# Memory attention on one core: scores and values issued by octets of heads instead of quads, exponentials a quad further ahead, and the projection chunks dealt anew

## The reference

```python
xn = layernorm(x) * ln_g + ln_b
q = heads(xn @ Wq); k, v = heads(xn @ Wkv)     # 16 heads of 64
mem = heads(ctx @ Wm)                          # 77 context rows
k = concatenate([k, mem]); v = concatenate([v, mem])   # 128 + 77 = 205 keys
attn = softmax(q @ k.T * 64 ** -0.5)
x = x + heads_joined(attn @ v) @ Wo + bo
```

## Time and profile before

| | |
|---|---|
| median of 3 runs | 3393.23 us (3392.61 to 3394.02) |
| the profiled execution, its span | 3395.16 us, 3393.4 us |
| memory attention | about 586 to 2014 us of the span |
| busy over the span: PE, DVE, ACT, POOL | 91%, 72%, 68%, 43% |
| busy in 640 to 1960 us: PE, DVE, ACT | 1299, 1017, 872 of 1320 us |

### The profile page before, as it was taken

How to read it: one execution, slowest core, us unless ns; L and a number is a source line. 1 busy time by engine, 2 the same in 40 slices (tenths; PEclk the granted TensorE clock), 3 DMA queues, 4 the chain that set the end, 5 groups by cost and what they waited for, 6 DMA issues and landing times. The chain is left out here.

```text
span 3393.4 us, 98827 instructions
## 1 busy us (share of the span) xinstructions
PE 3088.2 (91%) x27585; PEld 2273.9 (67%) x27741; DVE 2434.0 (72%) x8135; ACT 2315.4 (68%) x8950; POOL 1453.9 (43%) x2636
## 2 busy tenths in 40 slices
PE   7999997999999999999999968879979999968776
PEld 4555555788888888888888855657746666644444
DVE  6888886677777777777777751136657888868886
ACT  6888886666666666666666643337759999965554
POOL 5777775112222212222222210026647777746775
PEclk9999998999999999999999989989989999989999
DMA  4000001000000000000000002310000000000000
GB/s 147 0 0 0 0 0 58 23 4 5 5 5 5 5 5 5 5 3 5 5 5 4 4 5 81 83 49 18 17 9 7 5 6 5 5 3 7 12 17 14
DMA packets 80369, 54.43 MB, mean 16 GB/s; under 512 B 24801, under 2 KB 74413, under 8 KB 80160
## 3 DMA queue, kind: packets, MB, share of 16 engines
q1 hardware_dynamic: 76192, 45.27, 4.7%
q0 software_dynamic: 4096, 8.16, 0.8%
HBM read 32.67 MB, written 20.97 MB: 16 GB/s over the span
## 5 line engine op out<-in xcount | busy, mean ns | idle before, releaser
L873 DVE COPY b_prT<-b_tr 128x512 f32<-128x512 f32 x512 | 352.1, 688 | 237.8 <-PE b_tr L765 233.6
L1131 ACT ACTIVATE b_pr<-b_sc,b_low 128x205 f32<-128x205 f32 x1024 | 431.0, 431 | 33.9 <-DVE b_low L849 33.9
L461 ACT ACTIVATE a_pr<-a_sc,a_low 128x128 f32<-128x128 f32 x1024 | 360.8, 386 | 12.0 <-DVE a_low L364 7.2
L864 DVE TENSOR_SCALAR b_pn<-b_pr,b_rec 128x205 f32<-128x205 f32 x1024 | 298.8, 334 | 54.8
L1188 POOL TENSOR_TENSOR b_ln_var<-b_ln_mean_var,all_eps 128x1 f32<-128x1 f32 x64 | 12.1, 190 | 757.9 <-DVE b_ln_mean_var L140 757.9
L765 PE MATMUL b_tr<-all_ident,b_pn 128*128 128x128 f32 x2048 | 323.3, 281 | 5.3 <-DVE b_prT L873 3.1
L2108 ACT ACTIVATE f_pr<-f_sc,f_low 128x77 f32<-128x77 f32 x1024 | 320.2, 338 | 10.0 <-DVE f_low L1999 2.8
L500 POOL TENSOR_TENSOR a_pn<-a_pr,a_rec 128x512 f32<-128x512 f32 x256 | 261.2, 1042 | 123.4 <-DVE a_rec L372 106.7
L765 PEld LDWEIGHTS b_tr<-all_ident,b_pn 128*128 128x128 f32 x2048 | 227.5, 141 | 86.9 <-issue 78.8
L849 DVE TENSOR_REDUCE b_low<-b_sc 128x4 f32<-128x820 f32 x256 | 256.3, 1002 | 9.5 <-PE b_sc L753 9.5
L753 PE MATMUL b_sc<-b_kT,b_q 64*128 64x205 f32 x2048 | 247.1, 359 | 0.0
(11 more groups left out here) (302 smaller groups left out, 8494.7 us busy)
## 6 DMA issues: line engine op xcount, KB each, us to landing
scratch_x<-b_zeros SPq DMA_DIRECT2D x12, 512.0 KB, 5.0
e_xr<-scratch_x SPq DMA_DIRECT2D x24, 256.0 KB, 3.0
scratch_y<-e_yr SPq DMA_DIRECT2D x24, 256.0 KB, 2.4
all_X<-in_x SPq DMA_DIRECT2D x8, 512.0 KB, 6.9
e_w<-in_e_w SPq DMA_DIRECT2D x16, 256.0 KB, 3.1
out_x<-all_X SPq DMA_DIRECT2D x8, 512.0 KB, 3.2
w_mask<-in_mask SPq DMA_DIRECT2D x1, 2464.0 KB, 11.1
b_cT<-in_ctxT SPq DMA_DIRECT2D x32, 77.0 KB, 2.0
```

The lines of the kernel that those rows point to most:

```text
L461: op = act.activation(pr[:, g, u], sc[:, g, 128 * u:128 * u + 128], ACT.Exp, bias=low[:, g, u:u + 1], scale=-1.0, accum_out=sums[:, g, u:u ...
L864: op = dve.tensor_scalar(pn[:, j % 2, g, 0:KN], pr[:, j % 2, g, 0:KN], rec[:, j % 2, g:g + 1], None, ALU.mult)
L873: dve.tensor_copy(prT[:, j % 2, i].rearrange("p h t q -> p (h t q)"), tr[:]).then_inc(prT_made, 1)
L1131: op = act.activation(pr[:, j % 2, g, 0:KN], sc[:, j % 2, h, KN * i:KN * i + KN], ACT.Exp, bias=low[:, j % 2, g:g + 1], scale=-1.0, accum_ ...
```

## The change

Within the same stage, and with the same arithmetic:

- `score` takes an octet (two quads) at once and is issued twice a step instead of four times, in turns 0 and 2; it now waits until both quads in sc are exponentiated. `values` takes an octet too, also in turns 0 and 2.
- `exponentials` works two quads ahead instead of one, so b_low, b_sums, b_rec and b_pr have four buffers, as has b_prT.
- The values of an octet fill the whole bank b_pm (512 columns), and the projected output p_y is written into the first 128 columns of that bank, where it had columns of its own. `project_out` stands in turn 1 instead of turn 0, `residual` in turn 1 of VectorE, and the values of the next octet wait for it.
- `lowest` of both quads of an octet stands in turns 0 and 2, on either side of the second `divide`.
- The chunks are dealt anew, `place` moves ahead of the second k, and the router's `choose` moves from turn 2 to turn 1.

```diff
-        po, p_y = pm[:, 0:256], pm[:, 256:384]
+        po, p_y = pm, pm[:, 0:128]
...
-                  [("xT", 0), ("q", 0), ("k", 0), ("q", 1), ("k", 1), ("mv", 0), ("v", 0), ("v", 1), ("mv", 1),
-                   ("place", 0), ("rT", 0), ("rT", 1)]]
-
-        EARLY = [[[0, 1], [4, 5], [8], [11]], [[0], [], [4], []]]
-        LATE = [[[2, 3], [6, 7], [9, 10], [12, 13]], [[1], [2, 3], [5, 6], [7, 8, 9, 10, 11]]]
+                  [("xT", 0), ("q", 0), ("k", 0), ("q", 1), ("place", 0), ("k", 1), ("mv", 0), ("v", 0), ("v", 1),
+                   ("mv", 1), ("rT", 0), ("rT", 1)]]
+
+        EARLY = [[[], [2, 3, 4, 5], [], [9, 10, 11]], [[0], [2], [4], [6, 7]]]
+        LATE = [[[0, 1], [6, 7], [8], [12, 13]], [[1], [3], [5], [8, 9, 10, 11]]]
...
-                def score(b, p, j):
-                    n = NJ * b + j
-                    if due(2 * n - 2):
-                        pe.wait_ge(exped, 2 * n - 2)
...
+                def score(b, p, o):
+                    n = NJ * b + 2 * o
+                    if due(2 * n):
+                        pe.wait_ge(exped, 2 * n)
...
+                    for j in (2 * o, 2 * o + 1):
+                        for i in range(2):
+                            for h in range(2):
...
+                        last.then_inc(scored, 1)
...
                     for j in range(NJ):
                         transposes(b, j, 0)
+                        if j == 1 and not first:
+                            project_out(b - 1, 1 - p)
...
-                        if j > 0:
-                            values(b, p, j - 1)
-                        elif not first:
-                            values(b - 1, 1 - p, NJ - 1)
-                        if j < 2:
-                            score(b, p, j + 2)
-                        elif not last:
-                            score(b + 1, 1 - p, j - 2)
+                        if j == 0:
+                            if not first:
+                                values(b - 1, 1 - p, 1)
+                            score(b, p, 1)
+                        elif j == 2:
+                            values(b, p, 0)
+                            if not last:
+                                score(b + 1, 1 - p, 0)
                         transposes(b, j, 1)
...
-                        if j == 0 and not first:
-                            project_out(b - 1, 1 - p)
...
                         copy_probs(b, j, 1)
-                        if j < 2:
-                            lowest(b, j + 2)
-                        elif not last:
-                            lowest(b + 1, j - 2)
+                        if j == 0:
+                            lowest(b, 2)
+                        elif j == 2 and not last:
+                            lowest(b + 1, 0)
                         if j == 1 and not last:
                             move_context_keys(b + 1, 1 - p)
                         if more:
                             divide(nb, nj, 1)
-                        if j == 0 and inside(b - 1):
+                        if j == 0:
+                            lowest(b, 3)
+                        elif j == 2 and not last:
+                            lowest(b + 1, 1)
+                        if j == 1 and inside(b - 1):
                             residual(b - 1)
...
-                        more = j < NJ - 1 or not last
-                        nb, nj = (b, j + 1) if j < NJ - 1 else (b + 1, 0)
-                        if more:
+                        more = j < NJ // 2 or not last
+                        nb, nj = (b, j + 2) if j < NJ // 2 else (b + 1, j - 2)
+                        if more and j % 2 == 1:
                             exponentials(nb, nj, 0)
...
+                        if more and j % 2 == 0:
+                            exponentials(nb, nj, 0)
+                        if more and j % 2 == 1:
                             exponentials(nb, nj, 1)
                         if not last:
                             for k in LATE[1 - p][j]:
                                 copy_projection(b + 1, 1 - p, k)
+                        if more and j % 2 == 0:
+                            exponentials(nb, nj, 1)
```

More of the change, by code:

```diff
@@ L739, in project @@
                     last.then_inc(pj_made, 1)
-                def score(b, p, j):
-                    n = NJ * b + j
-                    if due(2 * n - 2):
-                        pe.wait_ge(exped, 2 * n - 2)
-                    if j == 0:
-                        pe.wait_ge(ck_moved, b + 1)
[L747 to L755, removed]
+                def score(b, p, o):
+                    n = NJ * b + 2 * o
+                    if due(2 * n):
+                        pe.wait_ge(exped, 2 * n)
+                    if o == 0:
+                        pe.wait_ge(ck_moved, b + 1)
+                    pe.wait_ge(pj_copied, chunk_end(b, p, "k", o))
+                    for j in (2 * o, 2 * o + 1):
+                        for i in range(2):
+                            for h in range(2):
+                                r = slice(XD * h, XD * h + XD)
+                                last = pe.matmul(sc[:, j % 2, h, KN * i:KN * i + KN], q[r, p, 2 * j + i],
+                                                 kT[r, p, 2 * j + i], start=True, stop=True, tile_position=(XD * h, 0))
+                        last.then_inc(scored, 1)
                 def transposes(b, j, i):
@@ L775, in values @@
                             pe.wait_ge(y_added, b)
[L776 to L784, removed]
+                    if due(2 * b + o):
+                        pe.wait_ge(oT_made, 2 * b + o)
+                    for j in (2 * o, 2 * o + 1):
+                        for i in range(2):
+                            c = 256 * (j % 2) + 128 * i
+                            for t, v in enumerate((vt, vm)):
+                                for h in range(2):
+                                    f = XD * (4 * j + 2 * i + h)
+                                    last = pe.matmul(po[XD * h:XD * h + XD, c:c + 128], v[:, p, f:f + XD],
+                                                     prT[:, j, i, h, t], start=t == 0, stop=t == 1,
+                                                     tile_position=(0, XD * h))
                     last.then_inc(pv_made, 1)
                 def project_out(b, p):
-                    pe.wait_ge(oT_made, NJ * b + NJ)
+                    pe.wait_ge(oT_made, 2 * b + 2)
                     for i in range(NP):
@@ L836, in _ @@
                 score(0, 0, 0)
-                score(0, 0, 1)
                 over_sequences(pe, step, **steps)
@@ L967, in between_copies @@
                             choose_best(b - 4)
[L968 removed]
+                        if j == 1:
                             choose(b - 4)
@@ L1008, in step @@
                             norm_statistics(dve, ln, X[:, b + 2], b + 2, p)
+                        if j == 2 and inside(b - 1):
+                            dve.wait_ge(r_seen, b)
                         if more:
@@ L1157, in step @@
                             weigh(b - 3)
-                        if j > 0:
-                            copy_out(b, p, j - 1)
-                        elif not (isinstance(b, int) and b == 0):
-                            copy_out(b - 1, 1 - p, NJ - 1)
-                        if more:
+                        if j == 0 and not first:
+                            copy_out(b - 1, 1 - p, 1)
+                        elif j == 2:
+                            copy_out(b, p, 0)
+                        if more and j % 2 == 0:
+                            exponentials(nb, nj, 0)
+                        if more and j % 2 == 1:
                             exponentials(nb, nj, 1)
@@ L1172, in _ @@
                     copy_projection(0, 0, k)
-                exponentials(0, 0, 0)
-                exponentials(0, 0, 1)
+                for j in range(2):
+                    for i in range(2):
+                        exponentials(0, j, i)
                 over_sequences(act, step, **steps)
```

66 lines of the change are left out of this document (31 added, 35 removed).

## The result

The changed kernel took 3721.86 us (median of 4 runs, 3720.93 to 3724.43) against 3393.61 us of the kernel before (4 runs, 3392.61 to 3394.02): ratio 1.0969, with a 95% interval of 1.0950 to 1.0988. It is slower, as forecast, but by 328 us instead of 245, and 22 us beyond the range. The profiled execution has a span of 3722.2 us.

A forecast was written before the change was run, and what follows sets the result against it. TensorE bounds the kernel before; with octets, stretches of 38.4 us plus 13.96 of octet blocks make 52.4 a pair against 43.9. Taking +7.9 over 31 pairs adds 245 to 3393: 3640 us, range 3560 to 3700.

The forecast's parts named there:

- A: Even step, first half, from scores' end to next values: VectorE's chain, values waiting for the residual; 8.5 us.
- B: Even step, second half, from scores' end to next values: ScalarE's chain of exponentials and chunk copies; 9.2 us.
- C: Odd step, first half, scores' end to next values: ScalarE's exponentials and copies, then logits and mk3; 10.5 us.
- D: Odd step, second half, scores' end to next values: ScalarE's exponentials and copies, with v chunks waiting; 10.2 us.
- V: TensorE's block of values for one octet: 1.89 us.
- S: TensorE's block of scores for one octet: 1.60 us.
- the middle: Growth per pair of steps taken between +7.3 us (hops of 0.05) and +8.5 us (hops of 0.23): +7.9 us.
- the hop: Time from the end of ScalarE's copy to TensorE's next matmul: 0.23 us from one row, bounded below by 0.05.
- the two ways of 0.2 to ScalarE: Time from TensorE's end to ScalarE's start, estimated as 0.2 us, ahead of the copies of mk3 and v0.
- Rival 2: Waits only half as long, as stretches catch up: +2.6 us a pair of steps, 3474 us; chance 0.09.
- rival 3: TensorE's clock falls behind pauses, once a pair of steps, costing 1.75 us each time: 3695 us; chance 0.10.
- Rival 1: TensorE stays the bound and the new waits don't arise, so joining quads saves time: about 3320 us; chance 0.05.

The follow-up runs named there:

- e1: The changed kernel with three unused matmuls of 512 columns added in each odd step, ahead of the output projection, mv 0 and v 0: 3645.50 us.
- e3: The changed kernel with VectorE's residual done before the norm statistics and divides of its turn, not behind them: 3677.19 us.
- e2: The changed kernel with ScalarE's copies of the chunks put ahead of the exponentials that wait for minima: 3541.64 us.
- e4: The changed kernel with the projection chunks dealt as before the change: 3624.24 us.
- e9: The kernel before with only the values taken by octets; output projection, residual and chunks left where they were: 3390.33 us, ratio 0.9991.
- e5: The changed kernel with e2 and e3 together, and on VectorE the second quad's minima behind the copy of the next turn: 3509.02 us.
- e7: The kernel of e5 with the chunks dealt as before the change, as in e4, one run: 3493.41 us.
- e8: The kernel before, still in quads, with exponentials a quad further ahead (four buffers) and behind all copies of the turn on ScalarE: 3393.67 us, ratio 1.0000.
- e6: The kernel before with values, outputs and residual in the changed kernel's form and places, scores still by quads, one v chunk moved: 3433.45 us.

## Why the prediction was right in direction and too small

**The sum of the stretches.** A 8.5 said, 8.40 measured. B 9.2 said, 9.04 measured. C 10.5 and D 10.2 said; 11.97 and 11.22 in the changed kernel, but 10.53 and 10.10 in e1, where the clock stays up. V and S 1.89 and 1.60 said, 1.90 and 1.59 measured. The predicted pair of 51.2 to 52.4 stands against 52.00 in e1, and the 51.8 of the forecast is near it. Against the steady 44.12 of before, that is +7.9 a pair, the predicted number, and e1's 3645.5 us lies 6 us from 3640.

That the middle came out is partly luck. In the changed kernel the hop from the end of ScalarE's copy to TensorE's next matmul is 0.05 us at the waits for the logits, mv and v (1236.74 to 1236.79; 1251.33 + 0.63 = 1251.96 to 1252.01), the lower bound and not the middle. By it the sum is about 51.5 us (51.2 only if the two ways of 0.2 to ScalarE shrink too), a half microsecond under the 52.00. In C two more errors cancelled: the logits wait also for the copy of mk 2, which the sum left out, and two mk copies took 1234.29 - 1233.68 = 0.61 us and not 0.9. (The terms of C ahead of the logits add up to 6.49 and not 6.45, which changes nothing.) What fills the half microsecond, which lies in C and D, was not traced.

The causes named for the stretches hold too: A waits for the residual in VectorE's queue (e3 took 0.5 of it), and B, C and D are ScalarE's queue (e2 brought them to 8.19, 9.34 and 8.76). Rival 2, waits half as long, is out with this: at full clock a pair grew by 7.9 us and not by 2.6.

**The step that failed is rival 3, the clock, which the sum put at nothing.** "My layout has single pauses of 1.6 us at most, so I give it 0.10", and "Once a pair, this would cost 1.75". The pauses were as said, at most 1.6 us, and the clock fell nonetheless, and twice a pair, in C and D. It cost 54.57 - 52.00 = 2.6 us a pair, in place of 1.75 if at all; over the stage 76 us. A fall costs less than I priced (1.65 in C and 1.11 in D by the pairs of e3), but there were two, in 27 of 28 steady pairs for C and in every one for D. The inference was drawn from one row, a single pause of 2.4 us. I took the length of that pause for what decides. It doesn't: in C the clock falls behind one pause of 1.53 us, in D behind 0.76, four records and 1.48; in B it stays up behind 1.21 and 0.55 (rows 1276 and 1278 above), and in e4 one and the same pause of 2.39 us brought it down in 22 pairs and not in 8. With other pauses than the one in the profile, no chance as low as 0.10 could be read from it. Rival 3 as I priced it gives 3695; with the 2.6 measured here it is 3640 + 31 x 2.6 = 3720, within 2 us of the result. This shows that the sum closes; it is no second forecast.

The Trainium skill's page "TensorE: Matmul & The Clock Gate", section "A second HAM failure mode: psum-queue depth-cycling", describes a clock that oscillates since TensorE idles in small pieces between groups of matmuls. This trace agrees in that the clock is at 0.50 behind waits of 0.76 to 1.53 us that come back in every pair. The section stands in the same Part 1 that the prediction names, which used only what Part 1 says of activity and idling.

**Rival 1 and the rule on tiling modes.** The joining did what it promised on TensorE: 0.50 us twice a sequence, with blocks of 1.90 and 1.59. The Trainium skill's "TensorEngine Tiling (Array Packing)", Key Properties (a change of mode drains TensorE), agrees with these lengths, though no run here shows the draining itself. It doesn't decide the time of the kernel: not even e9, which joins the values alone, was measurably faster.

**Where the 10.45 us a pair went.** Read as a chain of experiments, each from the steady pair:

| step | pair, us | worth |
|---|---|---|
| changed kernel | 54.57 | |
| clock kept up (e1) | 52.00 | 2.6 |
| ScalarE: copies ahead of waiting exponentials (e2) | 48.64 | 3.4 |
| VectorE: residual and second minima moved (e5) | 47.71 | 0.9 |
| chunks dealt as before (e7) | 47.17 | 0.5 |
| left over the kernel before | 44.12 | 3.1 |

The terms hang together: undone alone in the changed kernel, the deal is worth 3.4 us (e4) and not 0.5, and part of what e3 and e4 gained was clock. The last 3.1 us were not taken apart by an experiment. The waits say where they show up: 3.8 us a pair for VectorE's copies in e7, which the kernel before did not have, against the 2.0 that joining saves. The lead on exponentials cost nothing with quads (e8), and values by octets with their output and residual moved give 1.2 (e6: 45.31). My reading, not shown, is that they come from the head of 2.4 us behind each octet of scores, in which ScalarE has nothing and VectorE too much. A kernel with octets of scores and none of the rest wasn't tried: as long as scores are double buffered by quads, both quads must be exponentiated before the next octet, so the lead comes with it.

**Smaller points.** TensorE's busy share in the stage was said to be 80%; it is 86% (1419 of 1650), partly slow records. In e1 it is 84% without the added 78 us; each pause also has the modelled tail of the record before it counted as busy. That ScalarE would wait for the minima twice a sequence, 2 us or more each, was right (3.3). "Every other stage should be unchanged" was right. The waits came where they were expected (v, logits, values behind the residual), but for the one at xT, which the trace doesn't have; those at mv and at a transpose were not named.

## What to carry to other kernels

When TensorE is the bound and issues its work in small pieces for four other queues, joining pieces saves its fixed cost per piece, but makes the others idle and then crowded; work out each stretch's longest chain, with every copy that stands behind a waiting instruction in an in-order queue, before counting the saving. Put copies that TensorE waits for ahead of instructions that themselves wait for TensorE. And once TensorE gets pauses, look at the granted clock in short windows: give a fall of the clock a real chance, with its price, even if no single pause is long.

## What was not expected of the hardware

Adding work made a kernel faster: 93 matmuls of 0.86 us (186 more weight loads in the page) took 76 us off (3721.86 to 3645.50). The clock fell behind pauses of no more than 1.6 us, in nearly every pair. In C it fell when TensorE had been at work again for 1.6 us (idle to 1236.79, clock 1.00 up to 1238.38 and 0.50 from 1238.40), in D at once (idle to 1252.01, 1.00 up to 1252.03 and 0.50 from 1252.05). With pauses up to 1.3 us (e2) and up to 1.5 us (e7) it stayed at 1.00 from 640 to 1960 us. A pause of 2.39 us brought it down in 22 of 30 pairs of e4 and not in the other 8; this window of one of the 8 holds the pause and what follows (1236 to 1240 us, 1.61 us busy):

```profile
1236.00:1240.00 4.00, 1.61 (x11) 1.16 (x10) 3.79 (x12) 3.42 (x15) 0.00 (x0) 1.00 0.00 0
```

So the length of the longest pause alone doesn't tell whether the clock falls; what else decides was not measured here.
